# A mixture of experts over 64 experts: every expert on every token, against rows dispatched by expert and gathered back

## The reference

```python
logits = x @ gate_w.T                                  # x: layernorm of the tokens, [4096, 256]; 64 experts
topv, topi = jax.lax.top_k(logits, 8)
rw = jax.nn.softmax(topv, axis=-1)
W = jnp.zeros((N, E)).at[jnp.arange(N)[:, None], topi].set(rw)
gu = jnp.einsum('nh,eih->nei', x, gu_w)                # 64 gate and 64 up rows an expert
inter_w = silu(gu[..., :I]) * gu[..., I:] * W[:, :, None]
out = jnp.einsum('nei,ehi->nh', inter_w, dp_w)
sh_out = (silu(x @ sh_gate_w.T) * (x @ sh_up_w.T)) @ sh_down_w.T
out = out + sigmoid(x @ sh_gate1_w.T) * sh_out         # one shared expert for all
x = x + tanh(g_ffn[0]) * out
```

## Time and profile before

| | us |
|---|---|
| median of 3 runs | 1804.18 |
| lowest and highest | 1802.24 and 1805.04 |
| span of the profiled execution | 1802.4 |
| busy: PE, VectorE, ScalarE, GpSimd | 1656.9, 1164.4, 790.0, 877.7 |
| moved by DMA | 97.10 MB |

### The profile page before, as it was taken

The page is one execution under the profiler, slowest core; times in us unless marked ns, Lnnn a source line. Parts: engine busy times, 40 slices in busy tenths (PEclk is TensorE's granted clock), DMA queues, the critical chain, the costliest instruction groups (busy, mean ns, idle before and its releaser), DMA issues.

```text
span 1802.4 us, 29881 instructions
## 1 busy us (share of the span) xinstructions
PE 1656.9 (92%) x8726; PEld 854.0 (47%) x8736; DVE 1164.4 (65%) x2144; ACT 790.0 (44%) x1356; POOL 877.7 (49%) x1033
## 2 busy tenths in 40 slices
PE   6999998999999999999999999999987999956565
PEld 3566664444444444444444444444433666622232
DVE  7999995545444545445445445444456999958998
ACT  3555553434434434434334335334223555533553
POOL 7788981333332333332333333332324888845665
PEclk9999998999999999999999999999988999989676
DMA  9111111211221212221221222222310000000001
GB/s 227 53 45 51 52 44 55 69 65 62 65 71 58 67 64 61 66 68 61 64 64 61 69 59 67 64 58 71 114 53 10 1 0 0 0 1 0 24 23 47
DMA packets 64563, 97.10 MB, mean 54 GB/s; under 512 B 17856, under 2 KB 26240, under 8 KB 64128
## 3 DMA queue, kind: packets, MB, share of 16 engines
q1 hardware_dynamic: 64512, 96.48, 18.5%
HBM read 91.20 MB, written 5.24 MB: 54 GB/s over the span
## 4 chain that ended last, share of the span: by engine, by line
PE 82%; issue 5%; POOL 5%; DVE 5%; ACT 1%; DMA 1%; SPq 0%; POOLq 0%; DVEq 0%; ACTq 0%
PE bank L1201 37%; PE bank L1236 19%; PE bank L1075 9%; POOL region L486 4%; PE bank L1049 3%; PE bank L1063 3%; PE bank L1064 2%; PE bank L1116 2%; PE bank L1142 2%; PE bank L1129 2%; PE bank L1099 1%; DVE HM L984 1%; PE bank L1300 1%; DVE arena L753 1%; POOL region L473 1%
## 5 line engine op out<-in xcount | busy, mean ns | idle before, releaser
L1201 PE MATMUL bank<-arena,region 128*128 128x512 f16 x3072 | 707.9, 380 | 0.4 <-DVE arena L893 0.4
L443 POOL TENSOR_TENSOR arena<-arena 128x512 f16<-128x512 f32 x264 | 308.8, 1170 | 738.3 <-ACT arena L598 730.5
L917 DVE TENSOR_TENSOR arena<-bank,arena 128x512 f32<-128x512 f32 (+1 forms) x264 | 182.4, 691 | 438.3 <-PE bank L1201 420.5
L1201 PEld LDWEIGHTS bank<-arena,region 128*128 128x128 f16 x3072 | 298.4, 98 | 351.8 <-issue 8.1
L591 ACT ACTIVATE arena<-bank 128x512 f32<-128x512 f32 (+1 forms) x264 | 157.4, 597 | 583.5 <-PE bank L1201 583.0
L1236 PE MATMUL bank<-arena,region 128*128 128x512 f16 x1536 | 376.0, 381 | 13.4 <-POOL arena L443 13.4
L929 DVE TENSOR_TENSOR arena<-arena 128x512 f32<-128x512 f32 (+1 forms) x264 | 219.7, 832 | 44.5 <-DMA arena<-routing 28.9
L1236 PEld LDWEIGHTS bank<-arena,region 128*128 128x128 f16 x1536 | 149.9, 98 | 191.8 <-POOL arena L443 14.9
L1075 PE MATMUL bank<-arena 128*72 128x256 f32 (+1 forms) x768 | 187.8, 381 | 0.1
L598 ACT CAST arena<-arena 128x512 f16<-128x512 f32 (+1 forms) x264 | 161.1, 610 | 38.7 <-DVE arena L929 36.4
L753 DVE TENSOR_REDUCE arena<-bank 128x8 f32<-128x512 f32 x192 | 124.4, 676 | 10.6 <-PE bank L1049 6.7
(11 more groups left out here) (133 smaller groups left out, 1841.0 us busy)
## 6 DMA issues: line engine op xcount, KB each, us to landing
arena<-routing SPq DMA_DIRECT2D x512, 128.0 KB, 2.9
arena<-in_wpairs SPq DMA_DIRECT2D x32, 384.0 KB, 3.2
out<-arena SPq DMA_DIRECT2D x16, 256.0 KB, 2.2
...
x<-in_x SPq DMA_DIRECT2D x1, 1024.0 KB, 16.7
...
```

The source lines that it names most:

```text
L443: pool.tensor_tensor(IL[s % 3], IN[s % 2], IH[s % 3], ALU.subtract).then_inc(M["il_ready"], 1)
L917: dve.tensor_tensor(SL[s % 2][0:rows, :], bank[2 + s % 2][0:rows, :], SL[s % 2][0:rows, :], ALU.mult).then_inc(M["ut_done"], 1)
L1201: mm = pe.matmul(o, ww(k), xx[:, k, :], start=(n == 0), stop=(n == 3 * KT - 1))
```

## The change

The dense loop goes. Layer-0 attention stays, but the weights are laid out per expert (`RW`), each pair through five DMAs into another layout. After it comes a routing loop over 32 tiles: normalise, turn, logits, the eight largest, and for each of a token's eight experts its rank among the tokens of that expert, from a product with a triangular matrix (`ranks`); the shared expert is computed in the same loop. GpSimd scatters each tile's rows (high half, low half and routing weights: 640 16-bit values, 1280 B) eight times with an indirect DMA into a DRAM tensor `xs`, sorted by expert and rank. SyncE writes 128 rows of zeros behind each expert's last row. That is done in two halves of 2048 tokens with a tensor each. Then tables of 192 tiles of 128 slots per half tell which expert and which rows a tile has, and a loop of 96 groups of four tiles follows: `fetch` brings four tiles by transposing DMAs, `gate_up` and `down` use the expert's weights by a register's value, and `store` writes 512 rows of 256 32-bit values to `ys`. Layer-1 attention begins with `gathers`: GpSimd gathers eight rows per token by indirect DMAs, seven of which add into the buffer, and VectorE adds the sum to `x`. The loading and rounding of the last feed-forward's weights now stands between the experts and layer-1 attention. All three products per value stay.

```diff
-NWB = 4
...
+EW = 3 * H
+SW = KT * P + H
+EX1 = E + 1
+XW = 2 * H + 2 * E
+NHALF = 2
+HT = NT // NHALF
+HTOK = HT * P
+TILES = 192
+GT = 4
+NG = TILES // GT
+RING = 16
+NYA = 8
+RS = HTOK + P
+XROWS = E * RS + P
+YROWS = TILES * P
...
+            def pair(n, dst, done):
+                sp.dma_start(dst[0].rearrange("p m e i -> p (m e i)"), wpairs[:, bass.ds(n, 1), 0:KT * 2 * P].rearrange("p a w -> p (a w)")).then_inc(done, 16)
+                for e in range(2):
+                    for half in range(2):
+                        sp.dma_start(dst[1][half * I:(half + 1) * I, e, :], wpairs[e * I:(e + 1) * I, bass.ds(n, 1), KT * 2 * P:PW].rearrange("p a w -> p (a w)")).then_inc(done, 16)
...
-            def spread(c, back, ahead):
-                for s in range(NPAIR):
...
-                    for half in range(2):
-                        sp.dma_start(WB[s % NWB][half * I:(half + 1) * I, :],
-                                     routing[bass.ds(c, 1), 2 * s + half, :].to_broadcast([I, CH])).then_inc(d_wb[s % NWB], 16)
...
+            for h in range(NHALF):
+                sp.wait_ge(R_["cn"], 2 * h + 2)
+                for a in range(0, E, 8):
+                    _, v = nc.values_load_multi_w_load_instructions(FILL[0:1, h, a:a + 8], engines=[sp.engine], min_val=0, max_val=E * RS - P,
+                                                                    skip_runtime_bounds_check_because="an expert's rows and the P after them lie inside")
+                    for r in v:
+                        sp.dma_start(xs[h][bass.ds(r, P), :], ZERO).then_inc(d_fill, 16)
...
+            sp.wait_ge(R_["table"], TABLE_DONE)
+            sp.wait_ge(d_fill, 16 * NHALF * (E + 1))
+            for i in range(4):
+                sp.wait_ge(sent[i], 16 * 8 * NT // 4)
...
+            def fetch(g):
+                v = rows(g)
+                for q in range(GT):
+                    n = g * GT + q
+                    if n >= RING:
+                        sp.wait_ge(M["gu"], n - RING + 1)
+                    sp.dma_start_transpose(XR[n % RING], xs[g // NG][bass.ds(v[q], P), :]).then_inc(d_xr[g % 4], 16)
+            def store(g):
+                sp.wait_ge(M["ye"], g + 1)
+                sp.wait_ge(M["ya"], g + 1)
+                a = g % NG * GT * P
+                sp.dma_start(ys[g // NG][a:a + GT * P, :].rearrange("(q p) h -> p q h", p=P), YS[g % 2]).then_inc(d_ys[g % 2], 16)
+            for g in range(3):
+                fetch(g)
+            for g in range(NGG):
+                if g + 3 < NGG:
+                    fetch(g + 3)
+                store(g)
...
+            sp.wait_ge(M["dn"], NGG)
+            sp.dma_start(WF, wfc_in).then_inc(d_wf, 16)
+            sp.dma_start(WP, wproj_in).then_inc(d_wf, 16)
...
+                def gather(t, k):
+                    n = t % NYA
+                    if k == 0:
+                        if t >= NYA:
+                            pool.wait_ge(a["moe_in"], t - NYA + 1)
+                        pool.indirect_dma_start(YA[n], None, ys[t // HT], bass.IndirectOffsetOnAxis(ap=idx[:, t, k:k + 1], axis=0)).then_inc(d_ya[n], 16)
+                    else:
+                        pool.wait_ge(d_ya[n], 16 * (8 * (t // NYA) + k))
+                        pool.indirect_dma_start(YA[n], None, ys[t // HT], bass.IndirectOffsetOnAxis(ap=idx[:, t, k:k + 1], axis=0),
+                                                compute_op=ALU.add).then_inc(d_ya[n], 16)
...
+                def gathers(t):
+                    for part in range(2):
+                        for w in range(GT):
+                            if 0 <= t + w < NT:
+                                gather(t + w, 2 * (GT - 1 - w) + part)
...
+                    for t in range(-8, LAST[layer] + 1):
+                        gathers(t + 5)
+                        if t >= -3:
+                            step(t, t % 2)
...
-            def low(n, s):
...
-                pool.wait_ge(M["ih_ready"], n)
-                pool.tensor_tensor(IL[s % 3], IN[s % 2], IH[s % 3], ALU.subtract).then_inc(M["il_ready"], 1)
...
+            for s in range(NT + 2):
+                if s + 2 < NT:
+                    rstd(s + 2, (s + 2) % 4, 1)
+                if s >= 2:
+                    t = s - 2
+                    pool.wait_ge(R_["place"], place_at("index", t))
+                    pool.wait_ge(R_["place"], place_at("low", t))
+                    for k in range(8):
+                        pool.indirect_dma_start(xs[t // HT], bass.IndirectOffsetOnAxis(ap=at_row[t % 4][:, k:k + 1], axis=0), ROW[t % 4], None).then_inc(sent[t % 4], 16)
...
+            for g in range(NGG):
+                j = g % 2
+                pool.wait_ge(M["ih"], g + 1)
+                if g >= 2:
+                    pool.wait_ge(M["dn"], g - 1)
+                if g >= 1:
+                    pool.wait_ge(M["ih2"], g)
+                pool.tensor_copy(IH[j][I:P], IH[j][0:I]).then_inc(M["ih2"], 1)
...
+                    act.wait_ge(M["gu"], (g + 1) * GT)
+                    if g >= 2:
+                        act.wait_ge(M["in"], g - 1)
+                    act.activation(SL[j], bank[j][0:I, :], ACT.Silu).then_inc(M["sl"], 1)
...
+                    act.activation(YS[j][:, 2, :], yb[j][1][:, 0, :], ACT.Copy, scale=WS[j][:, 2:3])
+                    act.activation(YS[j][:, 3, :], yb[j][1][:, 1, :], ACT.Copy, scale=WS[j][:, 3:4]).then_inc(M["ya"], 1)
...
+                    act.copy(IH[j][0:I], IN[j].rearrange("p (q t) -> p q t", q=GT)).then_inc(M["ih"], 1)
...
-                        dve.wait_ge(whi_done, t + 1)
-                        dve.tensor_tensor(WL[:, bass.ds(t, 1), :].rearrange("p a w -> p (a w)"), stage[j],
-                                          WH[:, bass.ds(t, 1), :].rearrange("p a w -> p (a w)"), ALU.subtract).then_inc(wlo_done, 1)
+                        dve.wait_ge(whi_done, 2 * t + 2)
+                        dve.tensor_tensor(gu_view(t, SW), stage[j][0].rearrange("p m e i -> p e m i"), gu_view(t, 0), ALU.subtract)
+                        dve.tensor_tensor(RW[I:P, bass.ds(2 * t, 2), KT * P:SW], stage[j][1][I:P],
+                                          RW[I:P, bass.ds(2 * t, 2), KT * P:SW], ALU.subtract).then_inc(wlo_done, 1)
...
+                    if layer == 1 and inside(t + 4):
+                        dve.wait_ge(d_ya[(t + 4) % NYA], 16 * 8 * ((t + 4) // NYA + 1))
+                        dve.tensor_tensor(tile_x(t + 4), tile_x(t + 4), YA[(t + 4) % NYA], ALU.add).then_inc(a["moe_in"], 1)
...
+                dve.wait_ge(R_["place"], place_at("first8", t))
+                if t >= 4:
+                    dve.wait_ge(sent[t % 4], 16 * 8 * (t // 4))
+                dve.tensor_scalar(at_row[t % 4], p8[j], -1.0, None, ALU.add).then_inc(R_["place"], 1)
...
+            for s in range(NT + 3):
+                if s + 2 < NT:
+                    stats(s + 2, (s + 2) % 4, 1)
+                if s < NT:
+                    normalise(s)
+                if 0 <= s - 1 < NT:
+                    low(s - 1)
+                if 0 <= s - 3 < NT:
+                    shared_out(s - 3)
+                if 0 <= s - 2 < NT:
+                    shared_inner(s - 2)
+                    top(s - 2)
+                    shared_low(s - 2)
+                    shared_gain(s - 2)
+                if 0 <= s - 3 < NT:
+                    places(s - 3)
...
+                    dve.wait_ge(M["gu"], (g + 1) * GT)
+                    dve.wait_ge(M["sl"], g + 1)
+                    dve.tensor_tensor(IN[j], bank[j][I:P, :], SL[j], ALU.mult).then_inc(M["in"], 1)
...
+                    dve.tensor_tensor(YS[j][:, 0:2, :], yb[j][0], WS[j][:, 0:2].unsqueeze(2).to_broadcast([P, 2, H]), ALU.mult).then_inc(M["ye"], 1)
...
+                    dve.tensor_copy(WS[j], wb[j]).then_inc(M["ws"], 1)
+                    dve.wait_ge(M["ih"], g + 1)
+                    if g >= 2:
+                        dve.wait_ge(M["dn"], g - 1)
+                    dve.tensor_tensor(IL[j][0:I], IN[j].rearrange("p (q t) -> p q t", q=GT), IH[j][0:I], ALU.subtract).then_inc(M["il"], 1)
...
+            def split(o, lhs, rhs):
+                n = 0
                 for k in range(KT):
-                    mm = pe.transpose(bank[i][:, k * P:(k + 1) * P], DT[:, k, i * P:(i + 1) * P], ident)
-                mm.then_inc(M["ft_ready"], 1)
+                    for a, w in ((0, 0), (0, 1), (1, 0)):
+                        mm = pe.matmul(o, lhs(a, w, k), rhs(a, w, k), start=(n == 0), stop=(n == 3 * KT - 1))
+                        n += 1
...
+            def gate_up(g, v):
+                j = g % 2
+                if g >= 2:
+                    pe.wait_ge(M["in"], g - 1)
+                    pe.wait_ge(M["ws"], g - 1)
+                pe.wait_ge(d_xr[g % 4], 16 * GT * (g // 4 + 1))
+                for q in range(GT):
+                    u = (g * GT + q) % RING
+                    wx = RW[:, bass.ds(v[q], 1), :].rearrange("p a w -> p (a w)")
```

(23 more changed lines are left out.)

857 lines of the change are left out of this document (461 added, 396 removed).

## The result

The changed kernel takes 2462.8 us (median of 4 runs, 2461.3 to 2465.3) against 1803.3 us before: a ratio of 1.366, interval 1.364 to 1.368. It is 37% slower, where 4% was forecast, and 343 us above the upper end of the range. The profiled execution has a span of 2463.5 us.

What follows compares the result with a forecast made beforehand. The dense experts were taken as bound by TensorE's matmul columns, 1093 us to win back; 285 + 12 + 25 + 321 + 37 + 487 + 33 + 19 + 452 + 210 = 1881 us gave 1880 us, 4% slower, range 1640 to 2120 us.

Steps and rivals of the forecast that it cites:

- the joins: Between stages: TensorE idle about 40 us between routing and experts, and 50 between experts and attention.
- Then a tile takes GpSimd 8 x 1.16 + 0.75 = 10.0 us, above VectorE's 7.5.: Routing: eight scatters and one rstd make GpSimd the bound; 32 tiles take 321 us.
- c: GpSimd's time on one indirect DMA, scatter or gather: taken as 1.16 us, called the largest unknown.
- SyncE: five DMAs of 0.47 us, one register load and waits, 3.5 us.: Experts' stage: SyncE's load per group of four tiles, 3.5 us, below the DMA engines' 5.0 us.
- five candidates: Experts' group time: TensorE 2.2 to 4.4 us, chain 3.5, GpSimd/VectorE/ScalarE under 2.6, SyncE 3.5, DMA 5.0; highest binds.
- slow transposes: Rival, experts' stage: transposing reads at half the loads' rate, 7.2 us a group, plus 211 us, 2090 us; chance 0.10.
- T: Time of one group of four tiles in the experts' stage, 96 groups: 5.0 us, bounds 3.5 and 7.2.
- DMA share above 0.8: Sign for the forecast in the experts' stage, beside groups 5 us apart and TensorE's clock below 1.
- geometric middle: GpSimd's indirect DMA: 1.16 us, between SyncE's 0.468 us of issue and 2.9 us from issue to landing.
- cheap descriptors: Rival, routing and gathers: GpSimd's indirect DMA at 0.8 us, kernel faster at 1639 us; chance 0.38.
- The fill's 37 us: Zero rows for the second half, between routing and experts: 43 us of issue and loads, less 9, plus 3 of landing.
- c = 1.6 at 2105 us: Rival of dear descriptors, routing and gathers: 1.6 us per indirect DMA, plus 512 x 0.44, 2105 us; chance 0.10.

Runs made afterwards that it cites:

- e11: Changed kernel with five row buffers in routing instead of four: 2256.6 us.
- e12: Changed kernel with one transposing load per group of experts instead of four, all four tiles reading it: 2267.4 us.
- e13: Changed kernel with all 256 gathers bringing 64 rows instead of 128: 2404.2 us.
- e2: Changed kernel with ordinary DMAs of the same bytes instead of transposing ones for the experts' tile loads: 2356.7 us.
- e5: Changed kernel with each transposing load turning two blocks of 128x128 instead of five: 2419.8 us.
- e10: Changed kernel with two transposing loads of 256 rows per group, from fixed rows, instead of four of 128: 2380.4 us.
- e4: Changed kernel with the experts' stores issued by ScalarE instead of SyncE: 2406.1 us.
- e1: Changed kernel with eight row buffers and eight index buffers in routing instead of four: 2322.0 us.
- e8: Changed kernel with eight row buffers, stores from ScalarE, and plain gathers summed on VectorE: 2130.3 us.
- e15: e16 with the first half's 128 gathers issued during the second half's experts, adding straight into x: 1991.4 us.
- e16: e14 with five row buffers instead of eight: 2074.6 us.
- e17: e1 with one more one-column VectorE memset at the head of the last feed-forward: 2310.8 us.
- e14: e8 with the layer-1 key masks moved from GpSimd to VectorE: 2005.5 us.

## Why the prediction was wrong

Most mechanisms on the list were right: matmul columns no longer bound the experts, GpSimd bound attention, and the joins came out as priced. Three steps failed.

*"Then a tile takes GpSimd 8 x 1.16 + 0.75 = 10.0 us, above VectorE's 7.5."* The step took the highest of the engines' loads, as if each could run ahead of the others, and never asked how far. Four row buffers, with `high(s)` standing in program order ahead of the work for tile s - 3, let none run ahead at all: the parts add up to 17.3 us. e11 shows this, since one more buffer brings the tile to 10.95 us, and the scatters from the 530.5 us of e12 and e13 beside it to 349. The 10.95 us are the step's own sum with c at 1.266: 28 of the 215 us are the size of c, 187 the missing cycle.

*"SyncE: five DMAs of 0.47 us, one register load and waits, 3.5 us."* That is the price of an ordinary DMA, and a transposing one was given it. It is 1.20 us (0.333 us for an ordinary one in e2), so SyncE, not the DMA engines at 5.0 us, was the highest of the five candidates. e5, e10 and e4 show it from three sides: fewer bytes don't help much, fewer DMAs and fewer instructions in the queue do. The rival "slow transposes" has nearly the right T, 7.2, for another reason: it looked for the price in the engines' rate, and e5 has the DMA share at 0.44 with the group still at 6.6 us. The sign "DMA share above 0.8" came true, at 0.81, with groups 7.0 us apart, so it didn't name the bound. Two more of the five candidates were priced too low. Share times period gives the DMA engines 5.7 us a group in the changed kernel, 5.6 in e4 and 5.8 in e10, not 5.0. TensorE is busy for 4.5 us a group in e12 at a granted clock of 0.75, where 2.2 us at full clock would be 2.9 (an estimate). Behind the queue the engines are probably next, near 6 us, and then TensorE, near 5.2.

The Trainium skill, "Advanced Engine Details and Errata", section on the X-bar transpose, says that transposing DMAs are as fast as regular ones on trn2. The trace disagrees at this size: 7.00 against 5.90 us a group, 1.200 against 0.333 us of issue.

*"The time that GpSimd spends on one indirect DMA ...; call it c."* One c for two kinds. Scatters and plain gathers take 1.25 to 1.30 us with their gap, 0.1 above the value I chose; a gather that adds takes 1.85, and seven of eight in the attention add. A tile's gathers are 14.1 us instead of 9.3, GpSimd's own work 5.9 instead of 5.4. With the 28 or so tiles that are spaced by it this is some 146 of the 176 us (an estimate, 28 x 5.2); 36 gathers, not 28, stood ahead of the first step.

The geometric middle between 0.468 and 2.9 us was thus a good value for the plain kind, and the rival "cheap descriptors", at 0.38, got too much for a distance of 0.15 us. The Trainium skill, "DMA: Bandwidth & Descriptors", section on latency and other measured facts, puts the first byte of a DMA issued from GpSimd at about 1 us and calls it emission overhead; the 0.96 us here agree, the 1.55 us of a gather that adds don't, and I had weighed only what the Trainium skill says of where the 2 us go.

*Luck.* The fill's 37 us stood on 43 us of issue, of which 9 would be hidden, and 3 us of landing. Measured, the issue took 62.9 us, 21 of them were hidden behind the scatters, and 2 us followed: 44 us from the end of the last scatter, 39 of them behind the cut at 860. The two parts were 20 and 12 us off, and most of it cancels.

The sum over stages itself held: changes to three stages added up within 14 us. And the range missed for two reasons. The cycle and the queue were in no rival. And the rivals above, c = 1.6 at 2105 us and T = 7.2 at 2090, were each priced alone, while dear gathers and long groups came together.

*Open.* ScalarE's "remote" wait before the shared gate. It is in e1, e8, e15, e16 and e17 and not in e11 and e14, with five and eight buffers on either side; it costs 41 to 47 us of scatters. The kernels without it are just those of the set in which the fill is quick too, so it goes with the set rather than with the number of buffers, and the two together make 54 to 69 us (e17 and e1 against e11, e16 against e14). It isn't the chip, since e15 to e17 ran on the same one as e11 to e14, and the kernel before took 1803.6 us beside the one set and 1802.8 beside the other. The runs of one kernel agree within 19 us. What decides it was not found, and no kernel was run again in another set to see whether it changes sides.
